# A tuned one-core kernel of four layers: its prologue rebuilt, and two orders inside its block loop

## The reference

```
x = x + pool(softmax(mask(tanh(x W1 + b1) v))) / count         # layer 0, mask chosen by an id per row
x = x + attention(x) Wo + bo     # layer 1, 16 heads of 8; per row either dense with a bias, or over 32 gathered indices
h = relu(x wi + 2 (x cia) cib + 2 (x Ea[e]) Eb[e])             # layer 2, expert e of 8 per row, width 512
x = x + h wo + 2 (h coa) cob + 2 (h Oa[e]) Ob[e]
g = gelu(x fc1 + b)                                            # layer 3, width 512
x = x + concat(g fc2 + b2, g W3[e3] + b3[e3])                  # expert e3 of 16 per row
```

## Time and profile before

| | |
|---|---|
| median of 3 runs | 302.75 us |
| the profiled execution's own time / its span | 303.31 / 301.5 us |
| PE busy, share of the span | 269.0 us, 89% |
| DVE busy | 198.2 us, 66% |
| ACT / POOL busy | 130.7 / 116.6 us |
| start of `x1` of block 0 | 25.25 us |
| first matmul of step 1 that needs the low part of x2 | 63.45 us |
| one pass of the loop (`weigh(n, 2)` at 141.31 and 171.47) | 30.16 us |

### The profile page before, as it was taken

One profiled execution on the slowest core, in us unless ns is written; L12 is line 12 of the kernel. 1 busy time (PEld: TensorE's weight loads), 2 busy tenths in 40 slices (PEclk: granted clock), 3 DMA queues, 4 the chain that ended last, 5 costly groups with the idle time before them and its releaser, 6 DMA issues.

```text
span 301.5 us, 12584 instructions
## 1 busy us (share of the span) xinstructions
PE 269.0 (89%) x4861; PEld 198.3 (66%) x4861; DVE 198.2 (66%) x370; ACT 130.7 (43%) x220; POOL 116.6 (39%) x229
## 2 busy tenths in 40 slices
PE   8697999986889988998899889988998899978985
PEld 6384754545667766776677667766776677847854
DVE  3388695578767777777777777777777767473030
ACT  2033433224627452745274527452745265532231
POOL 7050049033542354235423542354235424560420
PEclk9859799999999999999999999999999999999999
DMA  5503970046305530553045304530553451055000
GB/s 174 185 4 135 282 215 2 0 139 227 130 2 174 214 142 4 174 209 139 0 174 209 139 0 176 207 139 0 177 205 139 187 210 60 35 213 192 22 0 37
DMA packets 26749, 38.25 MB, mean 127 GB/s; under 512 B 10577, under 2 KB 10833, under 8 KB 26594
## 3 DMA queue, kind: packets, MB, share of 16 engines
q1 hardware_dynamic: 26722, 37.87, 35.3%
HBM read 10.60 MB, written 2.10 MB: 42 GB/s over the span
## 4 chain that ended last, share of the span: by engine, by line
PE 42%; issue 24%; DVE 10%; POOL 10%; POOLq 10%; ACT 3%; DVEq 0%
PE pB L686 8%; POOLq L328 5%; PE pS L554 5%; POOL sc L310 5%; PE pB L746 4%; POOLq L338 3%; PE pB L719 3%; PE pB L714 3%; PE pB L644 2%; PE pV L630 2%; POOL x3b L318 2%; PE pB L640 2%; POOL rw L329 2%; PE pS L615 2%; PE pA L554 2%
## 5 line engine op out<-in xcount | busy, mean ns | idle before, releaser
L310 POOL TENSOR_TENSOR sc<-sc,rmax 128x512 f32<-128x512 f32 x32 | 33.6, 1050 | 83.6 <-DVE rmax L1024 83.6
L329 POOL COPY rw<-e3t_s 128x128 f32 x128 | 37.4, 293 | 52.2 <-issue 45.2
L439 ACT ACTIVATE ex<-sc 128x512 f32<-128x512 f32 x32 | 20.2, 631 | 44.8 <-POOL sc L310 44.5
L746 PE MATMUL pB<-rw,hT 128*32 128x128 f32 x1024 | 31.8, 274 | 0.4 <-ACT hT L447 0.4
L1030 DVE STREAM_TRANSPOSE pt<-ex 128x512 f32<-128x512 f32 x32 | 22.7, 708 | 14.2 <-ACT ex L439 14.0
L686 PE MATMUL pB<-rwo,hT 128*32 128x128 f32 x1024 | 29.8, 273 | 0.5 <-ACT hT L443 0.5
L1019 DVE SCALAR_TENSOR_TENSOR sc<-pS,bias 128x512 f32<-128x512 f32 x32 | 21.5, 671 | 12.1 <-PE pS L615 12.0
L644 PE MATMUL pB<-x_l,ffn_h 128*128 128x512 f32 x56 | 23.0, 411 | 7.0 <-DVE x_l L1077 5.8
L746 PEld LDWEIGHTS pB<-rw,hT 128*32 128x32 f32 x1024 | 27.3, 110 | 2.8 <-issue 2.2
L339 POOL COPY rwo<-weff 128x512 f32 x32 | 21.6, 680 | 18.6 <-ACT weff L461 9.6
L686 PEld LDWEIGHTS pB<-rwo,hT 128*32 128x32 f32 x1024 | 27.8, 110 | 1.1 <-ACT hT L443 1.1
(11 more groups left out here) (140 smaller groups left out, 522.1 us busy)
## 6 DMA issues: line engine op xcount, KB each, us to landing
...
```

Of the source, the lines that this page charges most:

```text
L310: pool.tensor_tensor(sc[:, g % 2, :, :], sc[:, g % 2, :, :], rmax[:, g % 2, :].unsqueeze(2).to_broadcast([P, H, S]), ALU.subtract).then_in ...
L329: pool.tensor_copy(rw[:, r, :, SHARED:D], e3t_s[:, bass.ds(e, 1), :, :].rearrange("p o c n -> p (o c) n"))\
L746: last = mm(pB2[S * q:S * q + S, P * g:P * g + P], hT[:, c, tok], rw[:, Q4 * g + q, c, :], start=(c == 0), stop=(c == FC - 1))
```

## The change

Loads: block 0's `xT` comes first on SP, then the 96 columns of `W1`, `xN`, the rest of the attention weights, `rank`, `ffn_w`, `e3t` and `fc2t`, with a semaphore for each use. The small loads, and later block 1's `xT` and `xN`, are issued by ACT. `poolP` is cleared by DVE instead of POOL.

Ids: wraps, the index table up to `idxm`, strengths and the expert masks go from DVE to POOL (21 small steps counted by `ids_sb`). The four copies of `bqk` go from POOL to ACT. POOL makes the low parts of the weights after the four `subtract_max` of block 0.

Order: on PE, `pooling`, `keys`, `queries` and `values` of block 0 come ahead of the low-rank products; 40 `keep_busy` matmuls ahead of `pooling` become 15. DVE makes `x1(0)` after the hit counts, and the products `W_O` and `W_I` after the first two `score_max`.

Expert products: four banks (`WOUT`) each first get wo's half (`base_out`), then `pairs_out` issues the pair products of the four row strips in turn, each into its own bank; twice, for the two halves of width.

In the blocks: `fc1` issues the high and low weight products of three chunks before it waits for `x_l`; DVE does `pool_weights(n+1, 1)` after `normalise(n, 0)` instead of ahead of `turn(n, 0)`.

```diff
+            sp.dma_start(attn_s[:, 0:A_Q], attn_w[:, 0:A_Q]).then_inc(ld_w1, 16)
             load_xN(0)
+            sp.dma_start(attn_s[:, A_Q:A_END], attn_w[:, A_Q:A_END]).then_inc(ld_attn, 16)
+            sp.dma_start(rank_s[:, :], rank_w).then_inc(ld_rank, 16)
...
-            load_x(1)
...
+            act.dma_start(ints_s[:, :], ints).then_inc(ld_ints, 16)
+            act.dma_start(cols_s[:, :], cols).then_inc(ld_cols, 16)
...
+            def next_x():
+                act.wait_ge(x1_sb, 1)
+                act.dma_start(xT[:, :], xt[1]).then_inc(ld_xT, 16)
+                act.wait_ge(pool_ps, 1)
+                act.dma_start(xN[:, :, :], xn[1]).then_inc(ld_xN, 16)
...
+            def pairs_out(half):
...
                 for c in range(2):
+                    for j in range(Q4):
+                        k = slice(S * j, S * j + S)
+                        first = P * (2 * half + c)
+                        last = mm(WOUT[j][:, 2 * P * c:2 * P * c + 2 * P], aT[k, first:first + P],
+                                  bpair[k, :, :], start=False, stop=(c == 1))
+                        if c == 1:
+                            last.then_inc(weff_ps, 1)
...
+            def fc1(i):
+
+                at(pe, x3_sb, 2 * (i + 1))
+                for c in range(FC - 1):
+                    if c == 2:
+                        at(pe, sc_sb, G * NBLK if isinstance(i, int) and i == NBLK - 1 else G * (i + 2))
+                    high, low_part = weight(N_FC1, c)
+                    mm(GIN[c][:, :], high, x3p[0][:, :], start=True, stop=False)
+                    mm(GIN[c][:, :], low_part, x3p[0][:, :], start=False, stop=False)
+                at(pe, x3l_sb, i + 1)
+                for c in range(FC - 1):
+                    mm(GIN[c][:, :], weight(N_FC1, c)[0], x3p[1][:, :], start=False, stop=True).then_inc(g_ps, 1)
+                parts3(GIN[FC - 1][:, :], weight(N_FC1, FC - 1), whole(x3p), True, True).then_inc(g_ps, 1)
...
             prepare_pooling()
-            prepare_hits()
-            wrap(I_E2, B, E2)
             pool_weights(0, 0)
+            pool_weights(0, 1)
             prepare_counts()
-            pool_weights(0, 1)
-            wrap(I_E3, B, E3)
-            prepare_ids()
             x1(0)
...
                     result(last)
-                if next_block:
-                    pool_weights(n + 1, 1)
                 turn(n, 0)
...
                 normalise(n, 0)
+                if next_block:
+                    pool_weights(n + 1, 1)
                 turn(n, 3)
```

More of the change, by code:

```diff
@@ new lines, in scorer_blocks, with indices @@
+            def scorer_blocks():
+                pool.memset(vblk[:, :], 0.0).then_inc(vblk_sb, 1)
+                pool.wait_ge(vblk_sb, 1)
+                pool.wait_ge(ld_scorer, 32)
+                for q in range(Q4):
+                    k = slice(S * q, S * q + S)
+                    pool.tensor_copy(vblk[k, k], scorer_s[k, 1:2].to_broadcast([S, S])).then_inc(vblk_sb, 1)
+                pool.wait_ge(vblk_sb, 1 + Q4)
+            def indices():
+                pool.wait_ge(ld_bools, 16)
+                step(pool.tensor_copy(mk[:, :], bools_s[:, :].bitcast(U8)))
+                pool.wait_ge(prep, P_INTS)
+                wrap(I_IDX, S, S)
+                step(pool.tensor_scalar(idxm[:, :], intf[:, I_IDX:I_IDX + S], 1.0, None, ALU.add))
+                step(pool.tensor_tensor(idxm[:, :], idxm[:, :], mk[:, S:2 * S], ALU.mult))
+                step(pool.tensor_scalar(idxm[:, :], idxm[:, :], -1.0, None, ALU.add))
+                assert ids_made[0] == IDS_IDX
@@ L703, in out_factor, with base_out @@
                 last.then_inc(aT_ps, 1)
-            def expert_out(u):
-                j, ps = u // 2, [pB1, pB2, pB0][u % 3]
-                if u == 0:
-                    pe.wait_ge(bpair_sb, 3)
-                    pe.wait_ge(aT_sb, 1)
-                at(pe, weff_sb, u - 2)
-                first = 2 * (u % 2)
+            def base_out(half, j):
+                if half == 0 and j == 0:
+                    pe.wait_ge(prep, P_WO)
+                if half == 0 and j == 1:
+                    pe.wait_ge(k_sb, 1)
+                if half == 0 and j == 2:
+                    pe.wait_ge(aT_sb, 1)
+                if half == 0 and j == 3:
+                    pe.wait_ge(prep, P_FBIAS)
+                if half == 1:
+                    pe.wait_ge(weff_sb, j + 1)
+                first = 2 * half
@@ L775, in _ @@
             scorer_in(0)
-            prepare_wi()
+            keep_busy(1, pS0, x2p[0])
             pe.wait_ge(vblk_sb, 1 + Q4)
             scorer_out(0)
+            keep_busy(6, pS0, x2p[0])
+            pooling(0)
+            pe.wait_ge(ld_attn, 16)
+            keys(0)
+            queries(0)
+            values(0)
+            pe.wait_ge(ld_rank, 16)
+            pe.wait_ge(ld_cols, 16)
+            prepare_wi()
             prepare_wo()
-            keep_busy(14, pS0, x2p[0])
-            pe.wait_ge(prep_pool, 2 + Q4)
@@ L782, in _ @@
-            pooling(0)
+            keep_busy(2, pS0, x2p[0])
+            scores(0, 0)
             prepare_last_bias()
-            queries(0)
-            keys(0)
-            scorer_in(1)
-            values(0)
-            out_factor()
-            keep_busy(4, pS0, x2p[0])
-            scores(0, 0)
-            keep_busy(4, pA0, x2p[0])
-            expert_out(0)
-            scorer_out(1)
-            scores(0, 1)
-            expert_out(1)
-            keep_busy(2, pA0, x2p[0])
-            weigh(0, 0)
@@ L798, in _ @@
-            expert_out(2)
-            expert_out(3)
-            keep_busy(2, pA0, x2p[0])
+            keep_busy(3, pA0, x2p[0])
+            base_out(0, 0)
+            base_out(0, 1)
+            scores(0, 1)
+            out_factor()
+            pe.wait_ge(v_sb, Q4)
+            scorer_in(1)
+            base_out(0, 2)
+            pe.wait_ge(th_sb, 2)
+            weigh(0, 0)
+            scorer_out(1)
+            base_out(0, 3)
+            pairs_out(0)
             weigh(0, 1)
-            expert_out(4)
@@ L857, in step_of @@
                 attn_out(n)
-                for c in range(FC):
-                    fc1(n - 1, c)
+                if last is None:
+                    pe.wait_ge(w_low, 3)
+                fc1(n - 1)
             step_of(1, None)
@@ L876, in _ @@
             keep_busy(4, pA0, ffn_p[0])
-            for c in range(FC):
-                fc1(NBLK - 1, c)
+            fc1(NBLK - 1)
             token_major(NBLK - 1)
```

250 lines of the change are left out of this document (132 added, 118 removed).

## The result

The changed kernel took 288.25 us (median of 4 runs, 287.84 to 289.89), the kernel before 302.36 on the same chip (4 runs, 299.57 to 302.86): ratio 0.9562, 95% interval 0.9491 to 0.9632. Run again beside later experiments it took 285.84 (6 runs, 283.58 to 288.57) against 301.18: 0.9508, 0.9471 to 0.9546. So the change is worth 14 to 15 us by the medians, not the 24.5 that were forecast, and 288.25 lies above the range (272.5 to 285.5).

A forecast was written before the change was run, and what follows sets the result against it. It took a serial chain with packed PE behind it to bound the prologue, PE's order and DVE's lateness the loop. Gains 11.85 + 0.7 + 1.7 + 10.3 = 24.5 off 303.31 gave 278.8, stated as 278; range 272.5 to 285.5.

The forecast's parts named there:

- the term of `weigh(n, 2)`: Loop: PE's wait for normalise shrinks once pool_weights moves, read from step 7; gain 0.39 us a pass.
- Small loads landed by 4.3: Prologue: at 0.45 us to issue a load, the first two loads on SP and on ACT land by 4.3.
- 13.4 for `x1(0)`: Prologue: x1(0) starts at 13.4 us instead of 25.25, a gain of 11.85.
- GpSimd steps of 0.3: Prologue: each small GpSimd id step of 32 elements takes 0.3 us, seven of them done by 10.3.
- the slower rival: GpSimd's 21 id steps delay PE's last-bias product; costs from 0.68 us a step, 316 at 2.5; chance 0.04.
- A round of 1.2: Expert products: one round of pair products takes 1.2 us, its four strips running side by side.
- 8.0 from `x1` to scores: Block 0 projections to first scores: 8.0 us instead of 8.7, clock low for part; gain 0.7.
- 26.0 from scores to low(0): First scores to x2's low part: 26.0 us instead of 27.7, gain 1.7; cases 26.45 with GpSimd's block, 24.85 without.
- the clock rival: PE's clock stays at 0.50 up to step 1, through fewer keep_busy and idle gaps: 291 us; chance 0.10.
- The hold of 1.6 for `l0r`: pool_weights(1, 1): GpSimd's weight lows and bias operations block DVE on the shared port, 1.6 us.
- The loop, 1.64 a pass: Each pass gains 1.64 us: fc1 0.5, weigh(n, 0) 0.75, weigh(n, 2) 0.39; five passes 8.2.
- Loop order lost: Rival: GpSimd blocks DVE's products, turn(n, 3) comes late and the order's 1.14 a pass goes: 285 us; chance 0.13.

The follow-up runs named there:

- e8: Changed kernel with the pair products of a round issued strip by strip instead of four strips in turn: 284.98 us, ratio 0.9498.
- e3: Changed kernel with pool_weights(n+1, 1) back ahead of turn(n, 0) on DVE: 292.99 us against 301.38 for the kernel before.
- e7: Changed kernel with GpSimd's three bias operations behind subtract_max(0, 1) and all tiles' token masks ahead of score_max(0, 2): 284.59 us, ratio 0.9462.
- e11: e10 with 22 more keep_busy matmuls, ahead of and behind pooling and ahead of the first base_out: 278.43 us, ratio 0.9248.
- e9: Changed kernel run once more, unaltered: 285.84 us, ratio 0.9508.
- e4: Changed kernel with the old fc1, each chunk's three matmuls together: 292.82 us, ratio 0.9731.
- e12: e10 without the 11 keep_busy matmuls behind scorer_out(0): 281.83 us, ratio 0.9357.
- e13: e10 with only the early fill, 14 keep_busy ahead of pooling and 9 behind it: 280.48 us, ratio 0.9284.
- e15: e11 with x1(0) between compare and reduction of the hit counts, and 4 keep_busy behind pooling instead of 9: 277.13 us, ratio 0.9173.
- e1: Changed kernel with 25 more keep_busy matmuls around pooling and ahead of the first base_out: 287.01 us, ratio 0.9547.
- e10: The combined kernel: changed kernel with vb cleared behind the expert ids, bulk loads held until small loads land, and bias operations moved: 281.15 us, ratio 0.9334.

## Why the prediction was wrong, point by point

Three steps failed. TensorE was at half clock behind the first scores, where the sum had it at full clock (3.0 of the 9.2 us that are missing). The way to `x1(0)` was 2.75 longer, by late loads and by a hold of DVE that was not charged there. And the term of `weigh(n, 2)` in the loop, 0.39 a pass, gave 0.04. Step by step:

- **Small loads landed by 4.3: wrong.** `ints` was near it (used at 4.45), `cols` came 1.0 late (5.37) and `W1` 0.8 (5.67); the scorer loads came at 6.4, where the prediction had their copies end at 5.9, and `bools`, which it did not price, at 8.3. It took a load by its issue, 0.45, from a trace with all the small loads first on one queue, and the change put a queue of bulk beside them. In this execution DVE did not wait for `bools`, as GpSimd's steps to the indices ended at 10.9 and the hits began at 11.77; but it pushed the `memset` onto `ctab` (see e8). In e3 and e7, where it landed 8.1 and 7.6 after its issue, DVE also waited 1.95 and 1.44 for the indices. Over the eight profiles with this order of loads and no hold, `x1(0)` moves with the landing of `bools`, from 14.7 (4.8 after issue) to 18.8 (8.3).
- **13.4 for `x1(0)`, 16.15 measured.** Of 2.75, 1.4 is the start: the weights of `scorer_in` came 0.8 late, the scorer copies (0.99 on GpSimd) held `scorer_out` for 0.7 more, and the transposes ended at 11.74 instead of 10.3. The other 1.3 is `ctab` and its neighbours, held by the `memset` (1.13 of it by `ctab`'s own row). The steps between are as forecast (1.30, 1.23, 1.22). The prediction knew the block and charged it in `pool_weights(1, 1)` alone, though the clearing of `vb` stood in its own sum for GpSimd.
- **GpSimd steps of 0.3: right, but for the one that DVE held.** They took 0.25 to 0.34 for 32 elements (one 1.38) and 0.45 to 0.75 for 128; the ids were done by 22.9, ahead of the product that needs them (26.68), so the slower rival had no ground.
- **A round of 1.2: right,** 1.08, in either order.
- **8.0 from `x1` to scores, 26.0 from scores to low(0): the work was right and the clock was wrong.** At full clock they are 5.75 and 24.8 (e11). With the hold in `pool_weights(1, 1)` the second is 26.4 (e3, e9). These are the prediction's own two cases, 24.85 and 26.45; its 26.0 lies between them, though it says that the 26.0 holds the whole 1.6. The changed kernel's profiled execution had 29.4, the hold of 1.5 in it. This is the clock rival, to which the prediction gave 0.10 and 291: bases of 2.08 and scores of 1.96 are as it described, but the clock came back at 39 and not only in step 1, and the time stayed under its 291. It is the largest single part, 3.0 of 9.2, and it changes between executions of one program: 283.58 and 288.57 with the same instructions.
- **The hold of 1.6 for `l0r`: right** (1.64 against 0.16, e7). That `cnt` (1.29 against 0.43 to 0.18) is held as well was missed.
- **The loop, 1.64 a pass: 1.30.** `fc1` 0.42 of 0.5 (0.40 by e4). `weigh(n, 0)` gained 0.80, forecast 0.75, and no wait is left. The term that failed is **`weigh(n, 2)`, 0.39: it gained 0.04.** The earlier trace rows were read rightly (4.70), but in a pass `weigh(n, 0)` to `out_rows` was 4.96 before (171.81, not 171.94) and is 4.92 after. Beside the wait for `normalise` stood ACT's last relu, which `out_rows` needs: before, it ended at 171.55, 0.26 ahead of `out_rows`; after, at 159.85, 0.25 ahead. So `out_rows` stood right behind the relu already, and the wait of 0.56 at `weigh(n, 2)` was time that PE would have waited for the relu. Step 7 was no model of a pass, as there `out_rows` starts 0.05 behind the relu in both kernels; step 7 is written out and the passes are a loop, but what makes the other 0.2 was not looked into. Together the order gave 0.84 by these segments and 0.88 by e3. The five passes took 144.8 (72.95 to 217.77) against 150.85, a gain of 6.0 of 8.2: 1.7 of what is missing is the 0.34 a pass, and 0.5 one pass of 29.41, in which `out_rows` took 4.27 instead of 3.70, with a gap of 0.20 that ends in nothing the profile shows; its cause is open. Step 1 gained 0.92 (17.68 to 16.76) of 1.43, step 7 its 0.7, and the end 0.5 that was not forecast.
- **Loop order lost: no.** `turn(n, 3)` is at 133.46 and is not waited for, with GpSimd holding `l0r` for 0.86 in a pass; this is hidden.

In sum 2.75 + 0.4 + 0.35 + 3.4 + 2.15 = 9.05 of the 9.2 between 278.8 and 288.02. Combining what the runs showed gives 277.13, near the number forecast, but by another way: through edits that the change did not have.

What sets the fall of the clock stays open. The one profile with no low stretch (e11) had gaps of at most 1.06 between its first matmul and step 1, and among the profiles of the combined kernel the bare one (e12) had the longest low stretches, 23 us in all; so filling works in the main. But e13 fell near 21.5 behind 14 us of nearly unbroken work, e15 at 21.9 behind 14 us in which the timeline shows no gap, and e1 at 25.0 behind 6.8 such us, while e10 and e9 idled 2.19 ahead of the first base and kept their clock. e3 and e9 fell once more at 53.3 and 50.5, just behind waits of 2.33 and 2.32 for `poolP`; the changed kernel's first profile has the same wait (2.33) and did not fall. Ahead of the falls of e1, e13 and e15 stood the low-rank products, with 16 rows of contraction, and the bias product of one column; e11 had the same ones at the same place and kept its clock, and no run changed them, so whether they play a part is untested. The Trainium skill, TensorE: Matmul & The Clock Gate, HAM oscillation — how this bites in real kernels, lays such falls to idle gaps of PE; e11 and e12 agree in direction, the second falls of e1, e13 and e15 do not.
